# Feed-forward: the last, partly filled inner tile computed as one half-and-half tile

## The reference

```python
HID = int(DIM * 4 * 2 / 3)            # DIM = 256, so HID = 682
...
h = shift_token(x)
mu = h.mean(-1, keepdims=True)
var = h.var(-1, keepdims=True)
h = (h - mu) / jnp.sqrt(var + 1e-05) * lg + lb
h = h @ w1 + b1                       # w1: 256 x 1364
a, g = jnp.split(h, 2, axis=-1)       # 682 value and 682 gate columns
h = a * jax.nn.gelu(g, approximate=False)
x = x + h @ w2 + b2                   # w2: 682 x 256
```

## Time and profile before

| | us |
|---|---|
| median of 3 runs | 2812.6 |
| profiled execution, its own time | 2808.05 |
| its span, first to last instruction | 2805.9 |
| feed-forward stage of layer 1, about | 1733 to 1955 |
| feed-forward stage of layer 2, about | 2555 to 2778 |
| PE busy over the whole span | 2517.2 (90%) |
| DVE busy | 2038.4 (73%) |
| ACT busy | 1559.1 (56%) |

### The profile page before, as it was taken

How to read it: one execution, slowest core, us unless ns; L and a number is a source line. 1 busy time by engine, 2 the same in 40 slices (tenths; PEclk the granted TensorE clock), 3 DMA queues, 4 the chain that set the end, 5 groups by cost and what they waited for, 6 DMA issues and landing times. The chain is left out here.

```text
span 2805.9 us, 66485 instructions
## 1 busy us (share of the span) xinstructions
PE 2517.2 (90%) x21520; PEld 1920.9 (68%) x21520; DVE 2038.4 (73%) x4559; ACT 1559.1 (56%) x3028; POOL 607.2 (22%) x702
## 2 busy tenths in 40 slices
PE   5699999999999993599999998998799999998995
PEld 4466766667666662477777776887577777776884
DVE  5699689959969994577777776665577777775666
ACT  2677567747747773365666564333456665663332
POOL 0000000000000001344444443222344444443122
PEclk7799999999999997799999999999899999999997
DMA  4400020020001004000000000000000000001003
GB/s 143 169 18 17 6 79 17 11 73 12 17 21 63 17 11 165 1 0 6 1 7 1 7 0 17 30 0 34 10 0 7 0 7 0 7 0 47 0 0 120
DMA packets 75105, 80.00 MB, mean 29 GB/s; under 512 B 4272, under 2 KB 67496, under 8 KB 73384
## 3 DMA queue, kind: packets, MB, share of 16 engines
q1 hardware_dynamic: 75048, 79.21, 8.5%
HBM read 58.23 MB, written 16.78 MB: 27 GB/s over the span
## 5 line engine op out<-in xcount | busy, mean ns | idle before, releaser
L504 ACT ACTIVATE at_p<-at_ps_s,at_shift 128x1024 f32<-128x1024 f32 (+3 forms) x384 | 335.9, 900 | 84.6 <-PE at_ps_s L636 44.9
L405 DVE TENSOR_TENSOR at_p_lo<-at_p,at_p_hi 128x1024 f16<-128x1024 f32 (+3 forms) x384 | 357.2, 951 | 5.5
L1126 ACT ACTIVATE ly_probs<-ly_masked,ly_small,ly_rq 128x256 f32<-128x256 f32 x512 | 302.4, 592 | 64.1 <-DVE ly_small L1312 63.3
L1510 PEld LDWEIGHTS ly_ps<-ly_values,ly_probs_T 128*128 128x128 f32 x2048 | 258.3, 191 | 15.3 <-issue 0.4
L1510 PE MATMUL ly_ps<-ly_values,ly_probs_T 128*128 x2048 | 259.7, 270 | 0.0
L1135 ACT ACTIVATE ly_probs_T<-ly_ps 128x512 f32<-128x512 f32 x256 | 150.6, 588 | 166.5 <-PE ly_ps L1510 149.5
L400 DVE CAST at_p_hi<-at_p 128x1024 f16<-128x1024 f32 (+3 forms) x384 | 206.1, 556 | 50.0 <-PE at_ps_o L662 24.8
L660 PE MATMUL at_ps_o<-at_v,at_p_hi 128*128 128x65 f16 x2304 | 237.7, 193 | 0.5 <-DVE at_p_lo L405 0.5
L661 PE MATMUL at_ps_o<-at_v,at_p_hi 128*128 128x64 f16 x2304 | 236.9, 194 | 0.0
L662 PE MATMUL at_ps_o<-at_v,at_p_lo 128*128 128x65 f16 x2304 | 235.8, 192 | 0.0
L660 PEld LDWEIGHTS at_ps_o<-at_v,at_p_hi 128*128 128x128 f16 x2304 | 210.7, 96 | 35.3 <-issue 26.6
(11 more groups left out here) (219 smaller groups left out, 6792.7 us busy)
## 6 DMA issues: line engine op xcount, KB each, us to landing
at_hT<-hT_hi SPq DMA_DIRECT2D x5, 1024.0 KB, 5.2
at_hT<-hT_lo SPq DMA_DIRECT2D x5, 1024.0 KB, 7.4
ly_a_raw<-in_ffn_wqkv SPq DMA_DIRECT2D x3, 1536.0 KB, 7.7
at_w_raw<-in_Wv SPq DMA_DIRECT2D x34, 128.0 KB, 2.1
at_w_raw<-in_Wq SPq DMA_DIRECT2D x34, 128.0 KB, 2.3
at_w_raw<-in_Wk SPq DMA_DIRECT2D x34, 128.0 KB, 2.3
n_x<-in_states SPq DMA_DIRECT2D x4, 1024.0 KB, 11.7
hT_hi<-n_hi SPq DMA_DIRECT2D x8, 512.0 KB, 3.0
```

Source lines behind the costliest of these rows:

```text
L405: dve.tensor_tensor(p_lo[u % P_RING][:, :, off:], probs[u % P_RING][:, :, off:], p_hi[u % P_RING][:, :, off:], ALU.subtract).then_inc(p_lo ...
L504: act.activation(probs[u % P_RING][:, :, off:], ps_s[u % 2][:, :, off:], ACT.Exp, bias=shift[:], scale=SCORE_SCALE).then_inc(exp_done, 1)
L1126: step = act.activation(pr[:, j % 2, h, :], sm[:, j % 2, h, :], ACT.Exp, bias=small[:, j % 2, 1, h:h + 1], scale=rq[:, par, 2 * j + h:2 * ...
L1510: step = pe.matmul(ps_pv[:, cols], pT[:, (2 * slot + h) * P:(2 * slot + h + 1) * P], vv[:, v_slots[slot], cols], start=(j == 0 and h == 0 ...
```

## The change

The 42 value columns and the 42 gate columns of the last inner tile now lie in one 128-column weight tile: values in columns 0 to 41, gates in columns 64 to 105, the rest zero. hidden(5) is then one product of 6 matmuls into bank 1 instead of two of 6 into banks 1 and 3. gelu(5) reads partitions 64 to 127 of that bank and writes partitions 0 to 63 of `gl`; `uf` and the high part are made on partitions 0 to 63. The low part is written to partitions 64 to 127 of the same tile that holds the high part, and the rows of w2 for these 42 columns are stored twice, at rows 0 and 64 of the last tile. With both parts stacked in one stationary tile, out(5) needs two matmuls per token tile (w2 high, w2 low) instead of three; this also adds the product low x low. The weight array is 1408 instead of 1536 columns per contraction tile, so the whole weight block is 4352 instead of 4608 columns, and a piece that POOL splits is 136 instead of 144.

```diff
+REST = HID - (HT - 1) * P
+HALF = P // 2
+W1_COLS = 2 * (HT - 1) * P + P
...
-        A_COLS, F_COLS = KT * 3 * INNER, KT * 2 * HT * P + HT * D
+        A_COLS, F_COLS = KT * 3 * INNER, KT * W1_COLS + HT * D
...
                 def gelu(n, i):
                     hold(act, s["tick"], (s["gu_mm"], at(2 * (n + i) + 2)), (s["uf_done"], at(n + i - 1)))
-                    act.activation(gl[:, i % 2, :], bank[2 + i % 2][:], ACT.Gelu, bias=b1[:, HT + i:HT + i + 1]).then_inc(s["gl_done"], 1)
+                    if i < HT - 1:
+                        act.activation(gl[:, i % 2, :], bank[2 + i % 2][:], ACT.Gelu, bias=b1[:, HT + i:HT + i + 1]).then_inc(s["gl_done"], 1)
+                    else:
+                        act.activation(gl[0:HALF, i % 2, :], bank[i % 2][HALF:P, :], ACT.Gelu,
+                                       bias=b1[HALF:P, HT + i:HT + i + 1]).then_inc(s["gl_done"], 1)
...
                 def u_high(n, i):
-                    act.activation(uT[:, 0, i, :], uf[:, i % 2, :], ACT.Copy).then_inc(s["u_hi"], 1)
+                    rows_of = slice(0, P if i < HT - 1 else HALF)
+                    act.activation(uT[rows_of, 0, i, :], uf[rows_of, i % 2, :], ACT.Copy).then_inc(s["u_hi"], 1)
...
                 def hidden_lo(n, i):
                     after(dve, "u_hi", n + i + 1)
-                    dve.tensor_tensor(uT[:, 1, i, :], uf[:, i % 2, :], f32(uT[:, 0, i, :]), ALU.subtract).then_inc(s["u_lo"], 1)
+                    if i < HT - 1:
+                        dve.tensor_tensor(uT[:, 1, i, :], uf[:, i % 2, :], f32(uT[:, 0, i, :]), ALU.subtract).then_inc(s["u_lo"], 1)
+                    else:
+                        dve.tensor_tensor(uT[HALF:P, 0, i, :], uf[0:HALF, i % 2, :], f32(uT[0:HALF, 0, i, :]),
+                                          ALU.subtract).then_inc(s["u_lo"], 1)
...
                 def hidden(n, i, par):
                     after(pe, "uf_done", n + i - 1)
+                    if i == HT - 1:
+                        cols = slice(2 * i * P, (2 * i + 1) * P)
+                        for k in range(KT):
+                            step = three_products(pe, bank[i % 2][:], w1[0][:, k, cols], w1[1][:, k, cols],
+                                                  fT_hi[:, par, k, :], fT_lo[:, k, :], k == 0, k == KT - 1)
+                        step.then_inc(s["gu_mm"], 2)
+                        return
...
                 def hidden_out(n, i):
                     after(pe, "u_lo", n + i + 1)
                     for t in range(CT):
+                        if i == HT - 1:
+                            for part in range(2):
+                                step = pe.matmul(bank[6 + t // 2][:, (t % 2) * D:(t % 2 + 1) * D], uT[:, 0, i, t * P:(t + 1) * P],
+                                                 w2[part][:, i, :], start=False, stop=(part == 1), skip_group_check=True)
+                            continue
```

More of the change, by code:

```diff
@@ L801 @@
 HT = -(-HID // P)
+REST = HID - (HT - 1) * P
+HALF = P // 2
+W1_COLS = 2 * (HT - 1) * P + P
+assert 0 < REST <= HALF
 QK_SCALE = 8.0
@@ L884, in phase_layers @@
         wqkv = [w[:, 0:KT * 3 * INNER].rearrange("p (k n) -> p k n", k=KT) for w in (a_hi, a_lo)]
-        w1 = [w[:, 0:KT * 2 * HT * P].rearrange("p (k n) -> p k n", k=KT) for w in (f_hi, f_lo)]
-        w2 = [w[:, KT * 2 * HT * P:KT * 2 * HT * P + HT * D].rearrange("p (k n) -> p k n", k=HT) for w in (f_hi, f_lo)]
+        w1 = [w[:, 0:KT * W1_COLS].rearrange("p (k n) -> p k n", k=KT) for w in (f_hi, f_lo)]
+        w2 = [w[:, KT * W1_COLS:F_COLS].rearrange("p (k n) -> p k n", k=HT) for w in (f_hi, f_lo)]
         SHIFT_TICKS = 32 * (B + 1)
@@ L963, in _ @@
                     sp.dma_start(wo, io["ffn_wo"][l].rearrange("(k p) n -> p k n", p=P)).then_inc(s["ld_wo"], 16)
-                    sp.dma_start(f_raw[:, 0:KT * 2 * HT * P].rearrange("p (k n) -> p k n", k=KT),
-                                 io["w1"][l].rearrange("(k p) a n -> p k (a n)", p=P)).then_inc(s["ld_ffn"], 16)
-                    sp.dma_start(f_raw[:, KT * 2 * HT * P:F_COLS].rearrange("p (k n) -> p k n", k=HT),
+                    sp.dma_start(f_raw[:, 0:KT * W1_COLS].rearrange("p (k n) -> p k n", k=KT),
+                                 io["w1"][l].rearrange("(k p) n -> p k n", p=P)).then_inc(s["ld_ffn"], 16)
+                    sp.dma_start(f_raw[:, KT * W1_COLS:F_COLS].rearrange("p (k n) -> p k n", k=HT),
                                  io["w2"][l].rearrange("(k p) n -> p k n", p=P)).then_inc(s["ld_ffn"], 16)
@@ L1362, in hidden_full @@
                     after(dve, "u_lo", n + i - 1)
-                    dve.scalar_tensor_tensor(uf[:, i % 2, :], bank[i % 2][:], b1[:, i:i + 1], gl[:, i % 2, :],
+                    rows_of = slice(0, P if i < HT - 1 else HALF)
+                    dve.scalar_tensor_tensor(uf[rows_of, i % 2, :], bank[i % 2][rows_of, :], b1[rows_of, i:i + 1], gl[rows_of, i % 2, :],
                                              ALU.add, ALU.mult).then_inc(s["uf_done"], 1)
@@ L1538, in hidden @@
                     after(pe, "uf_done", n + i - 1)
+                    if i == HT - 1:
[5 more added lines that the diff above has]
+                        return
                     for gate in range(2):
-                        cols = slice((gate * HT + i) * P, (gate * HT + i + 1) * P)
+                        cols = slice((gate * (HT - 1) + i) * P, (gate * (HT - 1) + i + 1) * P)
                         for k in range(KT):
@@ L1548, in hidden_out @@
                     for t in range(CT):
+                        if i == HT - 1:
[3 more added lines that the diff above has]
+                            continue
                         step = three_products(pe, bank[6 + t // 2][:, (t % 2) * D:(t % 2 + 1) * D],
                                               uT[:, 0, i, t * P:(t + 1) * P], uT[:, 1, i, t * P:(t + 1) * P],
-                                              w2[0][:, i, :], w2[1][:, i, :], i == 0 and t % 2 == 0, i == HT - 1)
+                                              w2[0][:, i, :], w2[1][:, i, :], i == 0 and t % 2 == 0, False)
                     step.then_inc(s["y_mm"], 1)
@@ L1706 @@
     w1, w2, b1 = arrays.pop("ffn_w1"), arrays.pop("ffn_w2"), arrays.pop("ffn_b1")
-    arrays["w1"] = np.zeros((L, D, 2, HT * P), w1.dtype)
-    arrays["w1"][:, :, :, :HID] = w1.reshape(L, D, 2, HID)
+    full = HID - REST
+    arrays["w1"] = np.zeros((L, D, W1_COLS), w1.dtype)
     arrays["w2"] = np.zeros((L, HT * P, D), w2.dtype)
     arrays["w2"][:, :HID] = w2
+    arrays["w2"][:, full + HALF:full + HALF + REST] = w2[:, full:]
     b1_pad = np.zeros((L, 2, HT * P), b1.dtype)
-    b1_pad[:, :, :HID] = b1.reshape(L, 2, HID)
+    for gate in range(2):
+        part = w1[:, :, gate * HID:(gate + 1) * HID]
+        arrays["w1"][:, :, gate * full:(gate + 1) * full] = part[:, :, :full]
+        last = 2 * full + gate * HALF
+        arrays["w1"][:, :, last:last + REST] = part[:, :, full:]
+        bias = b1[:, gate * HID:(gate + 1) * HID]
+        b1_pad[:, gate, :full] = bias[:, :full]
+        b1_pad[:, gate, full + gate * HALF:full + gate * HALF + REST] = bias[:, full:]
     arrays["b1_col"] = np.ascontiguousarray(b1_pad.reshape(L, 2 * HT, P).transpose(0, 2, 1))
```

## The result

The change made the kernel slower. Over 11 runs each the median went from 2811.24 us (2806.67 to 2813.36) to 2819.64 us (2812.91 to 2821.66), a ratio of 1.0029 (95% interval 1.002 to 1.0039). The forecast was 2808.7, its range ended at 2814.0. The profiled execution took 2819.15 us, its span 2817.0 against 2805.9. The work did shrink: from the page of the kernel after,

The account below looks back on a forecast made before the run. PE was taken to bound the stage (busy 26.54 of 27.00 us), with a second chain ending nearly together. Gains of 14 x 0.21 = 2.9 and 2 x 0.48 = 1.0, 3.9 off 2812.6, gave 2808.7 us, range 2804 to 2814.

Parts of the forecast that it names:

- Hidden(5) costs and gives nothing: At hidden(5): six matmuls fewer, 1.37 us, do not start gelu(5) earlier; PE's wait before out(5) grows from 0.41 to 1.78.
- The prediction's own sign for this: At PE's new wait: the forecast is wrong if matmuls behind it follow at 0.43 us instead of 0.23.
- Rival 1: At PE's new 1.78 us wait: the clock falls, 1.4 us a fall, gain gone from three falls; chance 0.15.
- the rival's case of all 14 chunks falling (2828): In the full chunks: one clock fall in each of 14 adds 19.6 us to 2808.7.
- The 0.08 us of chunk_lo: On DVE: chunk_lo's 0.08 us overlap with the low part goes, cutting the gain from 0.29 to 0.21 us a chunk.
- I take no change, also where input and output lie in different halves: Tile 5's four links on ACT and DVE: on 64 partitions they keep their times of 0.70, 0.75, 0.63 and 0.69 us.
- eight matmuls as worked out: At out(5): eight matmuls instead of twelve end 0.48 us earlier, then chunk_lo is late next; 0.29 us gained before overlap loss.
- 0.05 from another pair of instructions: At hidden(0): PE starts 0.05 us after chunk_lo ends, as out(5) did after the low part (1786.63 to 1786.68).
- The forecast of 14 x 0.21 = 2.9 us: In the 14 chunks followed by a hidden(0): each 0.21 us shorter, 2.9 us in all.
- The last chunks: At each layer's last chunk, with no hidden(0) behind it: out(5)'s whole 0.48 us comes through, 1.0 us for two.
- POOL and the weights' DMA: Weight split and load: POOL saves at most 0.045 us a tile, hidden; the DMA, 6% shorter, gives nothing.

Follow-up runs that it names:

- experiments 1 to 3: Changed kernel with six unused matmuls (2809.83 us) or three (2809.2); kernel before with gelu(5) delayed by two unused ScalarE instructions (2828.68) or three (2844.92).
- r1_filler: Changed kernel with six unused matmuls more ahead of hidden(5), so PE's work is that of before: 2809.83 us, ratio 1.0.
- r7_filler3: Changed kernel with three unused 512-column matmuls more ahead of hidden(5): 2809.2 us, ratio 0.9993.
- experiment 5: Changed kernel with tile 5's low part back at partition 0 and out(5) as 12 matmuls over 64 partitions: 2832.76 us, ratio 1.0082.
- Experiment 6: Changed kernel with value and gate columns swapped, so gelu(5) reads and writes partitions 0 to 63: 2818.05 us, ratio 1.0027.
- r4_early: Changed kernel with the next chunk's chunk_full and chunk_hi issued on ScalarE ahead of gelu(4): 2785.62 us, ratio 0.991.

## Why the prediction was wrong

- **Hidden(5) costs and gives nothing: half right, and the step that failed.** Gelu(5) did not start earlier, and PE's wait took up the 1.37 us. But "This part of the change I cost at nothing" left out what the wait does to the clock. The wait of 1.89 us (1.78 forecast, and ACT's 0.14 of below) brought a half-clock stretch in 6 of 14 chunks, 1.17 us each: +7.0 us, by experiments 1 to 3. The prediction's own sign for this came true there: matmuls behind the wait follow at 0.43 us (1818.05 to 1818.48). Rival 1 had this mechanism and nearly this price (1.4 us a fall, break-even at three), but I gave it 0.15, because the trace had 1.00 after 1.51 us and 0.50 after 2.12, and my sum put the wait between them. Between a length that is harmless and one that is not, even chances were due; and the rival's case of all 14 chunks falling (2828) was not how it went. The Trainium skill ("TensorE: Matmul & The Clock Gate", section "A second HAM failure mode: psum-queue depth-cycling") tells of a kernel whose clock went up and down because of short idle times between groups of matmuls. The changed kernel's trace agrees with it in 6 of 14 chunks, r1_filler (0.53 us a chunk) and r7_filler3 (1.2 us) do not, and I had given it too little weight.
- **The 0.08 us of chunk_lo: the right mechanism, 0.11 in size.** Chunk_lo starts 0.72 us behind the low part's start, at or behind its recorded end, against 0.61 before, and the 0.61 came back in experiment 5. The Trainium skill's rule ("VectorE: DVE Perf Modes", section "Two Vector instructions with no wait between them"), by which an instruction whose output begins in another group of 32 partitions than the output ahead waits until the earlier ones have finished, is borne out by this.
- **"I take no change, also where input and output lie in different halves": wrong by 0.14 us a chunk.** The durations held. But I looked for the price in how long gelu(5) takes, and it stood in when it starts: with its input in the upper half, it no longer overlaps the end of chunk_hi. Experiment 6 gave the 0.14 back. The row needed was there, since gelu(5) began 0.12 us before chunk_hi's end, just as chunk_lo did on DVE.
- **Out(5): eight matmuls as worked out,** 0.48 us less on PE, with chunk_lo late next, as forecast. PE started 0.14 us after chunk_lo's end where I had 0.05 from another pair of instructions (0.05 holds for out(5) behind the low part still). The 0.09 is not explained; it is the same in r4_early and r1_filler.
- **The forecast of 14 x 0.21 = 2.9 us** so became 14 x -0.02 = -0.3.
- **The last chunks:** from gelu(4) to the addition to the stream 8.78 us instead of 9.14 in layer 1, and 8.77 instead of 9.14 in layer 2: 0.36 and 0.37 of the 0.48. ACT's 0.14 lies ahead of it there too.
- **Sum by the measured terms:** in the full chunks +7.4 (7.0 of it falls), in the two last chunks -0.7: +6.7, where the medians say +8.4. The profiled pair has +11.1, with 2.9 of the output phase, 1.3 ahead of the feed-forward stages and 0.2 between the layers, none of which the prediction had and none of which any run ties to the change. How many of the timed executions had the long output phase, or another number of falls, is not known, so the other 1.7 us stay unassigned.
- **POOL and the weights' DMA** cost and gave nothing that shows: POOL's busy time went from 607.2 to 603.1 us, with no wait for it at a chunk's end, and 2.0 of these 4.1 are its one addition in the output phase (6.52 against 4.55).

## What to carry to other kernels

Work taken from an engine that then waits is not free on TensorE: write down the length of the idle time that the edit makes, compare it with the longest that the trace shows without a fall of the clock, and count what lies beyond as possibly costly, with a chance of its own. When two chains end together, shorten both in one edit: here the smaller product and the earlier order gave almost nothing each, and 1.58 us a chunk together. When an operand moves to other partitions, compare the instruction's start with the end of the one ahead, not its duration. And before you read a difference of two profiles as the change's, cut both at the same instructions and see whether pieces that the change doesn't touch differ too: here one did, by 2.9 us.

## What the runs showed that I had not expected

- Whether one of many equal idle times is followed by a half-clock stretch varies from chunk to chunk: none of 14 chunks at 0.41, 0.53, 1.2 and 1.45 us, 7 of 13 at 1.75, 6, 7 or 8 of 14 at 1.89, 6 of 14 at 2.40.
- The overlap of neighbours on ScalarE, 0.12 to 0.13 us, goes when gelu(5) reads from partition 64 (1.47 us from start to start against 1.32), with the output's partition unchanged.
- Six superfluous matmuls in the idle time bought back about 10 us in the medians, 7.0 of them in the chunks.
- Half-clock stretches lasted about 3.4 us in most cases and 6.4 to 6.7 us in seven; twelve matmuls over 64 partitions went with six of the seven.
- In the output phase, POOL's addition starting about 0.1 us ahead of DVE's instead of behind it went with a first store 4.3 us later and an end 2.9 us later.
